# The lag of the weighting in an attention loop that streams over key blocks: 4 or 3 units by position, or a constant 4

## The reference

```
WINDOW = 16; heads H = 16, HD = 16
blocked[i, j] = (j <= i) & (j >= i - WINDOW)
def attention(x):                       # on layernorm(x)
    q, k, v = split(x @ in_proj_weight.T + in_proj_bias)
    scores = (q / sqrt(HD)) @ k.T
    scores = where(blocked, -inf, scores)
    return softmax(scores) @ v @ out_proj_weight.T + out_proj_bias
def ffn(x):                             # on layernorm(x)
    return tanh(x @ weight @ aux_weight1 @ aux_weight2 + bias)
x = x + attention(layernorm(x))
x = x + ffn(layernorm(x))
```

## Time and profile before

| | |
|---|---|
| median of 3 runs | 2017.15 us (2016.45 to 2018.87) |
| time of the traced execution | 2016.49 us |
| its span | 2014.8 us, 1.7 us less than its time |
| ScalarE busy | 1927.0 us, 96% |
| TensorE matmul busy | 1822.5 us, 90% |
| VectorE, GpSimd busy | 703.0 us (35%), 153.7 us (8%) |
| DMA | 93.76 MB, mean 47 GB/s |
| granted TensorE clock | 0.992 over the span |

### The profile page before, as it was taken

The page is one execution under the profiler, slowest core; times in us unless marked ns, Lnnn a source line. Parts: engine busy times, 40 slices in busy tenths (PEclk is TensorE's granted clock), DMA queues, the critical chain, the costliest instruction groups (busy, mean ns, idle before and its releaser), DMA issues.

```text
span 2014.8 us, 100136 instructions
## 1 busy us (share of the span) xinstructions
PE 1822.5 (90%) x46728; PEld 752.1 (37%) x46728; DVE 703.0 (35%) x1415; ACT 1927.0 (96%) x2113; POOL 153.7 (8%) x178
## 2 busy tenths in 40 slices
PE   7799999999999999999999999999998978888895
PEld 4333343343434334343343434334342323223232
DVE  6233343433444343343434334343432212121123
ACT  4599999999999999999999999999999999999994
POOL 2000000101010010101101000010100000000001
PEclk9899999999999999999999999999999999999998
DMA  4400111101231110102221111211022010000101
GB/s 132 140 26 27 47 33 55 42 22 47 65 93 33 53 43 17 58 25 64 63 63 52 28 57 30 59 38 42 21 67 66 22 42 22 25 30 12 42 14 44
DMA packets 93448, 93.76 MB, mean 47 GB/s; under 512 B 17562, under 2 KB 84570, under 8 KB 93026
## 3 DMA queue, kind: packets, MB, share of 16 engines
q1 hardware_dynamic: 92772, 87.05, 14.8%
q10 hardware_dynamic: 256, 0.26, 0.1%
HBM read 52.56 MB, written 25.72 MB: 39 GB/s over the span
## 4 chain that ended last, share of the span: by engine, by line
ACT 54%; issue 29%; PE 15%; DMA 1%; DVE 1%; SPq 1%; POOL 0%; DVEq 0%
ACT probs L1220 53%; PE outs L1287 7%; PE scores L1268 4%; PE ps_qk L487 2%; ACT s_pre L1212 1%; PE ps_v L504 1%; PE spare L1370 1%; SPq L155 0%; PE spare L1315 0%; PE spare L1326 0%; PE ps_turn L457 0%; DMA inverse<-row_inverse 0%; DMA xin<-in_x 0%; PE spare L1302 0%; PE scores L1475 0%
## 5 line engine op out<-in xcount | busy, mean ns | idle before, releaser
L1220 ACT ACTIVATE probs<-scores 128x1024 f32<-128x1024 f32 x2048 | 1887.3, 1112 | 22.5 <-PE scores L1268 20.4
L1287 PE MATMUL outs<-probs,vs 64*32 64x512 f32 x16384 | 1077.1, 590 | 0.0
L1268 PE MATMUL scores<-qs,ks 49*32 49x512 f16 x16384 | 840.2, 383 | 158.8 <-ACT probs L1220 143.8
L1268 PEld LDWEIGHTS scores<-qs,ks 49*32 49x32 f16 x16384 | 233.8, 89 | 1079.2 <-ACT probs L1220 1044.2
L1287 PEld LDWEIGHTS outs<-probs,vs 64*32 64x32 f32 x16384 | 302.3, 106 | 35.7 <-issue 10.5
L886 DVE TENSOR_TENSOR probs<-probs,allowed 128x320 f32<-128x320 f32 (+2 forms) x280 | 147.5, 530 | 337.6 <-ACT probs L1220 337.4
L1326 PE MATMUL spare<-s_xt,w_qkv 64*32 64x256 f32 x3072 | 120.7, 375 | 0.0
L828 POOL TENSOR_TENSOR s_squares<-s_qk_f 128x512 bf16<-128x512 f32 x48 | 61.3, 1278 | 384.5 <-DVE s_qk_f L957 384.5
L822 POOL TENSOR_TENSOR s_x<-s_x,bias_o 128x1024 f32<-128x1024 f32 x16 | 38.2, 2385 | 573.7 <-DMA s_x<-in_x 573.7
L954 DVE TENSOR_SCALAR s_qk_f<-spare,bias_qk 128x512 f32<-128x512 f32 x48 | 36.1, 751 | 129.8 <-PE spare L1326 129.8
L1016 DVE TENSOR_TENSOR s_x<-s_x,spare 128x512 f32<-128x512 f32 x30 | 20.7, 688 | 171.5 <-PE spare L1326 171.5
(11 more groups left out here) (119 smaller groups left out, 786.6 us busy)
## 6 DMA issues: line engine op xcount, KB each, us to landing
qs<-q_parts SPq DMA_DIRECT2D x192, 64.0 KB
ks<-k_parts SPq DMA_DIRECT2D x192, 64.0 KB
inverse<-row_inverse SPq DMA_DIRECT2D x32, 256.0 KB
s_x<-in_x SPq DMA_DIRECT2D x16, 512.0 KB, 5.6
ctx_in<-raw SPq DMA_DIRECT2D x248, 32.0 KB, 2.0
out<-s_pre SPq DMA_DIRECT2D x15, 512.0 KB, 3.5
s_xin<-in_x SPq DMA_DIRECT2D x12, 512.0 KB, 6.3
q_parts<-s_parts SPq DMA_DIRECT2D x24, 256.0 KB, 2.3
```

What stands on the lines that cost most here:

```text
L1220: act.activation(probs[:, u % RING, 2 * slot:2 * slot + 2].rearrange("p c q -> p (c q)"), scores[:, 2 * slot:2 * slot + 2].rearrange("p c ...
L1268: last = pe.matmul(scores[cols, 2 * slot + e], ks[rows, group, keys], qs[rows, group], start=True, stop=True)
L1287: last = pe.matmul(outs[32 * c:32 * c + 32, side], vs[keys, at:at + 2 * HD], probs[keys, u % RING, c], start=(i == 0), stop=(i == KBLOCKS ...
```

## The change

`weighed_at` now gives the unit 4 back at every place, and nothing else. So places 0 to 3 weight the last four units of the pass before, place 3 has a weighting, and no unit has two. At place 4, where the first weighting of a pass falls, the order is score, score, weighting, and no piece. After the last unit four weightings are left instead of three.

Pieces are moved by one unit where the new order wants it: away from place 4 (units 36 and 68), and into place 45, which was without one. `evacuate` goes from places 3 and 35 to 4 and 36, `invert` from 8 and 40 to 9 and 41, `scale_context` of the first pass from 45 to 46, `normalise` from 4 and 5 to 5 and 6, the Tanh (`SQUASH_AT`) of a chunk that runs beside a projection from 72 to 73. What is computed stays the same.

```diff
-TURN_AT = (7, 8, 9, 10)
-QK_AT = ((12, 14, 15, 16), (18, 19, 20, 21), (33, 34, 35, 36), (38, 39, 40, 41))
+LAG = 4
+TURN_AT = (8, 9, 10, 11)
+QK_AT = ((13, 14, 15, 16), (18, 19, 20, 21), (33, 34, 35, 37), (39, 40, 41, 42))
-V_AT = ((43, 44, 46, 47), (51, 52, 53, 54))
+V_AT = ((44, 45, 46, 47), (51, 52, 53, 54))
-F_AT = {True: ((61, 62, 63, 64), (66, 67, 68, 69)), False: ...}
-SQUASH_AT = {True: 72, False: 58}
+F_AT = {True: ((61, 62, 63, 64), (66, 67, 69, 70)), False: ...}
+SQUASH_AT = {True: 73, False: 58}
         def weighed_at(position):
-            i = position % KBLOCKS
-            base = position - i
-            if i < 3:
-                found = [base - 3 + i]
-            elif i == 3:
-                found = []
-            elif i < 13:
-                found = [position - 4]
-            elif i == 13:
-                found = [position - 4, position - 3]
-            else:
-                found = [position - 3]
-            return [u for u in found if 0 <= u < NCH * STEP]
+            return position - LAG if 0 <= position - LAG < NCH * STEP else None
...
-                    if finishes and r == 3:
+                    if finishes and r == LAG:
                         evacuate(f, 1)
-                    if r == 35:
+                    if r == KBLOCKS + LAG:
                         evacuate(step, 0)
-                    if r == 40:
+                    if r == KBLOCKS + LAG + 5:
                         invert(step, 0)
-                    if r == 45:
+                    if r == KBLOCKS + LAG + 10:
                         scale_context(step, 0)
...
-                        if r in (4, 5):
-                            normalise(step, r - 4)
+                        if r in (5, 6):
+                            normalise(step, (5, 6).index(r))
...
-                        if r == 8:
+                        if r == LAG + 5:
                             invert(f, 1)
...
+                    due = weighed_at(u)
                     score(u, 0)
-                    due = weighed_at(u)
-                    if due:
-                        weigh(due[0])
+                    if due is not None and r % KBLOCKS != LAG:
+                        weigh(due)
                     score(u, 1)
-                    for w in due[1:]:
-                        weigh(w)
+                    if due is not None and r % KBLOCKS == LAG:
+                        weigh(due)
...
-            for u in range(NCH * STEP, NCH * STEP + 3):
-                for w in weighed_at(u):
-                    weigh(w)
+            for u in range(NCH * STEP - LAG, NCH * STEP):
+                weigh(u)
```

More of the change, by code:

```diff
@@ L48 @@
 STEP = HALVES * KBLOCKS
-TURN_AT = (7, 8, 9, 10)
-QK_AT = ((12, 14, 15, 16), (18, 19, 20, 21), (33, 34, 35, 36), (38, 39, 40, 41))
+LAG = 4
+TURN_AT = (8, 9, 10, 11)
+QK_AT = ((13, 14, 15, 16), (18, 19, 20, 21), (33, 34, 35, 37), (39, 40, 41, 42))
 FOLD_AT = (23, 28)
 Y_AT = ((23, 24, 25, 26), (28, 29, 30, 31))
-V_AT = ((43, 44, 46, 47), (51, 52, 53, 54))
+V_AT = ((44, 45, 46, 47), (51, 52, 53, 54))
 NORM_AT = 49
 F_TURN_AT = {True: (56, 57, 58, 59), False: (41, 42, 43, 44)}
-F_AT = {True: ((61, 62, 63, 64), (66, 67, 68, 69)), False: ((47, 48, 49, 50), (52, 53, 54, 55))}
-SQUASH_AT = {True: 72, False: 58}
+F_AT = {True: ((61, 62, 63, 64), (66, 67, 69, 70)), False: ((47, 48, 49, 50), (52, 53, 54, 55))}
+SQUASH_AT = {True: 73, False: 58}
 SCALE_UP = 1024.0
```

## The result

The changed kernel takes 2014.07 us (median of 10 runs, 2011.84 to 2016.55) against 2017.58 us (10 runs, 2015.37 to 2020.65) for the kernel before: ratio 0.9975, with a 95% interval of 0.9967 to 0.9984. The two medians alone lie 3.51 us apart, 0.17%. The interval leaves out no change, so the kernel is faster, by 0.16% to 0.33%; that it is faster by more than 0.2% is not shown by this measurement. The traced execution took 2012.43 us, 4.06 less than the one of before.

A forecast was written before the change was run, and what follows sets the result against it. It took ScalarE's exponentials as the bound, with time lost to late starts that overlap hides. Terms -6.7, +1.2, +0.2 and +0.9 summed to -4.4 us: 2012.7 us against the median, range 2010.5 to 2016.0.

The forecast's parts named there:

- the double unit: The unit with two weightings in each pass: removing it wins 0.21 us in each of 32 passes, -6.7 us.
- The limit of 1.21: A unit's second scores may begin up to 1.21 us after its due time for nothing; only what is beyond costs.
- +1.2 for the first weighting: First weighting behind the second scores: unit 37's second scores 1.25 after due time, 0.04 us lost in 31 passes.
- the place that is paid back: Rival: the first weighting's two waits or dense pieces cost 0.13 a pass, +4.0 instead of +1.2, 2015.5 us; chance 0.11.
- the free place 5: Rival: overlap hides 0.04 more at place 5 and pauses fall well, -5.6 and below, 2011.0 us; chance 0.12.
- The evacuation, 0.29 to spare: VectorE's two copies after a pass's last weighting are done 0.29 us before the next first weighting begins, cost 0.
- The first pass, +0.2: Units 4 and 5 at the 1.2 GHz clock: delay handed to unit 5, +0.2 us, between -0.3 and +0.5.
- The end, +0.9: After the last scores a fourth weighting runs before VectorE copies, with nothing beside it: +0.9 us.
- Nothing was lost: Rival: by the idle column the steady part has nothing to give, only the end counts, 2018.0 us; chance 0.05.
- Pauses, ±1.5: TensorE pauses where nothing is waited for may fall otherwise in another program: ±1.5 us allowed.

The follow-up runs named there:

- The repeated run: The changed kernel run again without any change, beside the follow-up kernels: 2011.88 us (11 runs), ratio 0.9974 to the kernel before.
- lag 3: The changed kernel with a constant lag of 3 instead of 4, run twice: 2012.77 us (ratio 0.998) and 2014.53 us (ratio 0.9989).

## Why the prediction was right, point by point

It said 2012.7 us, 0.22% less; measured are 2014.07 and 2011.88, by the ratios 0.25% and 0.26% less than before, by the medians 0.17% and 0.25%.

The repeated run gives the cleanest sum, since its exponentials keep the distance of before. From the first to the last they take 1899.9 us, 6.6 less than before. The losses at the double unit (-6.7), at units 5 and 37 (+1.5) and in step 0 (+0.2) and the pauses (-1.6) make -6.6. The stretch behind the last exponential is 1.6 longer, and the traced execution 5.0 shorter (2011.49 against 2016.49). That the first trace came so near to the -4.4 (-4.06) is in part luck: the pauses gave it 1.7 us, and its slower pace of 0.9175 took 1.6 back.

**The double unit, -6.7.** Right. Before, 0.21 were lost in both passes of every step. Now nothing is, and four value pieces in a row (units 44 to 47) cost nothing.

**The limit of 1.21, and +1.2 for the first weighting.** Right: second scores came 1.26 after due time (said: 1.25), and 0.05 a pass were lost (said: 0.04), which makes +1.5. The two waits of the first weighting cost nothing. That settles the rival of the place that is paid back; the free place 5 falls too.

**The evacuation, 0.29 to spare.** Right to the hundredth, and the run with the weighting between the scores shows what is behind it: 0.59 a pass.

**The first pass, +0.2.** At units 4 and 5 of step 0 1.48 us were lost before, and 1.35 and 1.67 in two traces after. In six traces with this order it is 1.35 to 1.85: always the same 1.16 at exponential 5.0 (before, at 4.1), and 0.19 to 0.69 at 5.1, where before lost 0.32. Against the one trace of before that is -0.1 to +0.4, within my bounds of -0.3 to +0.5; its sign stays open. The window at the half clock, changed kernel:

```profile
81.00:86.80 5.80, 4.83 (x64) 1.46 (x72) 2.04 (x9) 4.75 (x7) 1.22 (x2) 0.52 0.92 290
```

**The end, +0.9.** Right: from the start of the last scores to VectorE's copy it is 3.97 against 3.11 before, 0.86 more. What comes behind scatters by as much: from the last exponential to the end of the span it is 32.97 in one trace of the changed kernel and 34.00 in the other. It isn't the transfers: up to the copy behind them (`ctx_in`) it is 12.88 and 12.83. It is the matmuls after that copy, the first trace and then the second:

```profile
1991.37 3.58 PE scores L1463 x8
```
```profile
1989.36 5.50 PE scores L1463 x12
```

TensorE had next to nothing to do during the transfers. The granted clock is 0.50 (the 1.2 GHz level) from 1991.37 to 1993.20 in the first trace and rises within the 1.75 us that follow (mean 0.61); in the second it is still 0.50 from 1989.36 to 1993.20. The prediction has no term for this.

**Nothing was lost** (the idle column) falls. It is also measured how far that column misleads: of a loss of 0.10 it shows nothing, of one of 0.31 it shows 0.21. The Trainium skill, "Perfetto Trace Analysis", section "Identifying the Most-Contended Engine", calls occupancy a fair measure of how near ScalarE is to its roofline. It is 96% in both kernels, so it doesn't show what could be won here.

**Pauses, ±1.5.** That pauses fall otherwise in another program was right, the size too small. In steps 1 to 15 they took 4.1 us before, 2.4 and 2.5 after, and 1.7 to 8.7 over all the kernels. So -1.6 of the gain in the second trace is no work of the lag; the terms that are (-6.7, +1.5, +0.2 and +0.9) add up to -4.1 instead of the -4.4 forecast. The ten runs of before lie within 5.3 us, not within 2.4 as the three that the prediction knew. At this size the pauses decide whether the change passes 0.2%, and they can't be read from the order of the work.

## What to carry to other kernels

Where ScalarE seems full, measure the distance between the ends of its instructions, not its idle time: a short duration is a hidden late start, and here 0.12 us of it are free and the rest costs in full. Give each unit of the other engine a due time and add up its order from that; it told to 0.01 us what a repeated group would do and to 0.04 what the move of a whole weighting would. It failed where the length of a group was guessed: half of the matmuls of a weighting took as long as all of them. For gains below some 5 us in a long unrolled program, look at where pauses of TensorE fall before you believe a verdict on the order.

## What was not expected of the hardware

- TensorE's pauses come at fixed distances in its instruction stream (187 to 193 modulo 256, 0.3 to 1.7 us each), and many come back at the same instruction in the next trace: the two traces of lag 3 both paused at number 7105 (1.64 and 1.62 us) and at 11201 (0.56), those of the changed kernel at 43969 (0.73 and 0.80) and 48577 (0.83 and 0.98). Not all do: 50625 paused in the first of these (0.71) and not in the second. The Trainium skill, "Runtime: NRT & Kernel Launch", section "Instruction fetch mechanics", says that instructions come in blocks of 256 by the sequencer's own DMA queue, and that crossing a block is mostly hidden. The distance agrees. Hidden it mostly is, but not always: what is left was 1.7 to 8.7 us a run. Blocks pause only where their packet landed late, 1.2 to 1.8 us before (3.2 in the median elsewhere). Why these packets are late, and why others as late show no pause, stays open.
- A weighting by half of its column groups took as long as a whole one (1.03 against 1.04 us); by half of its queries it took 0.62.
- One run of the same program had exponentials every 0.9175 us and another every 0.9167, 1.6 us over the kernel.
